# A two-layer graph network with experts on one Trainium2 core: the order around two reductions, and the first expert's first weights fetched for all experts

## The reference, cut to what matters

```python
kp = prm_exp(k, w)
qp = prm_exp(q, w)
D = jnp.einsum('btm,bm->bt', qp, jnp.sum(kp, axis=1))[..., None]
kptv = jnp.einsum('btn,btm->bnm', v, kp)
y = jnp.einsum('btm,bnm->btn', qp, kptv) / (D + EPS_ATTN)
y = v + (y @ proj_w + proj_b)
h2 = layernorm(y, n2_g, n2_b)
```

```python
logits = x @ Wg + bg
w, idx = jax.lax.top_k(logits, K)
w = jax.nn.softmax(w, axis=-1)
h = jax.nn.silu(jnp.einsum('bsh,ehf->ebsf', x, W1) + b1[:, None, None, :])
y = jnp.einsum('ebsf,efh->ebsh', h, W2) + b2[:, None, None, :]
comb = jnp.einsum('bske,bsk->ebs', jax.nn.one_hot(idx, E, dtype=x.dtype), w)
return jnp.einsum('ebsh,ebs->bsh', y, comb)
```

## Time and profile before

| | us |
|---|---|
| median of 3 runs | 827.68 |
| the three runs | 823.75, 831.24, 827.68 |
| profiled execution, device time | 823.53 |
| its span, first to last instruction | 821.7 |
| PE busy in the span | 792.5 (96%) |
| DVE busy | 533.9 (65%) |
| ACT busy | 251.2 (31%) |
| POOL busy | 142.5 (17%) |
| mean granted TensorE clock | 0.983 of full |

### The profile page before, as it was taken

The page is one execution under the profiler, slowest core; times in us unless marked ns, Lnnn a source line. Parts: engine busy times, 40 slices in busy tenths (PEclk is TensorE's granted clock), DMA queues, the critical chain, the costliest instruction groups (busy, mean ns, idle before and its releaser), DMA issues.

```text
span 821.7 us, 10813 instructions
## 1 busy us (share of the span) xinstructions
PE 792.5 (96%) x3983; PEld 634.0 (77%) x3983; DVE 533.9 (65%) x731; ACT 251.2 (31%) x488; POOL 142.5 (17%) x106
## 2 busy tenths in 40 slices
PE   5999999999999999999999999999599999999997
PEld 4998758766577776577858778898499989888886
DVE  6867999999999999985878445078531111511112
ACT  4452214245211014024143442133432321432310
POOL 3100010220200000001301620032342420442400
PEclk9999999999999999999999999999599999999999
DMA  7601789796987876711053110000342130423001
GB/s 247 235 1 52 223 250 347 219 273 217 255 325 252 276 246 232 233 58 50 1 165 104 53 51 0 1 1 1 103 161 95 52 103 0 135 70 102 0 0 62
DMA packets 60339, 107.89 MB, mean 131 GB/s; under 512 B 4065, under 2 KB 13662, under 8 KB 60300
## 3 DMA queue, kind: packets, MB, share of 16 engines
q1 hardware_dynamic: 54636, 96.97, 35.3%
q0 software_dynamic: 2880, 5.12, 3.8%
q10 hardware_dynamic: 2784, 5.27, 1.7%
HBM read 103.51 MB, written 1.28 MB: 128 GB/s over the span
## 4 chain that ended last, share of the span: by engine, by line
PE 93%; DVE 3%; issue 1%; ACT 1%; DVEq 0%; POOL 0%; DMA 0%; POOLq 0%; SPq 0%
PE bank L1341 55%; PE bank L1799 14%; PE bank L1410 6%; PE bank L1560 4%; PE bank L1579 3%; PE bank L1572 2%; PE bank L1553 2%; PE bank L1348 2%; PE bank L1667 2%; PE bank L1459 1%; PE bank L1742 1%; PE bank L1545 0%; ACT slot L617 0%; DVE tmp L953 0%; DVE slot L968 0%
## 5 line engine op out<-in xcount | busy, mean ns | idle before, releaser
L1040 DVE SCALAR_TENSOR_TENSOR weights<-weights,att 128x2048 f32<-128x2048 f32 x116 | 263.5, 2344 | 0.7
L1322 DVE CAST hid_hi<-slot 128x626 fp32r<-128x626 f32 x32 | 15.7, 492 | 159.2 <-ACT slot L894 159.2
L1341 PE MATMUL bank<-half,ew_hi 128*128 128x314 f32 (+1 forms) x512 | 112.9, 310 | 2.2 <-POOL ew_lo L586 2.2
L1341 PE MATMUL bank<-AT,slot 125*128 125x312 f32 (+1 forms) x400 | 105.8, 426 | 0.0
L1341 PEld LDWEIGHTS bank<-AT,slot 125*128 125x128 f32 x400 | 75.6, 189 | 30.4 <-issue 1.3
L586 POOL TENSOR_TENSOR ew_lo<-weights,ew_hi 128x1024 fp32r<-128x1024 f32 x28 | 69.2, 2492 | 133.3 <-ACT ew_hi L876 133.3
L1341 PEld LDWEIGHTS bank<-half,ew_hi 128*128 128x128 f32 x512 | 87.4, 191 | 5.6 <-issue 2.9
L1341 PE MATMUL bank<-weights,slot 128*125 128x512 f32 (+5 forms) x306 | 84.4, 437 | 0.7 <-ACT slot L775 0.7
L894 ACT ACTIVATE slot<-bank,eb_now 128x312 f32<-128x312 f32 x64 | 33.4, 523 | 155.3 <-PE bank L1341 155.3
L1341 PE MATMUL bank<-half,ew_lo 128*128 128x312 f32 (+1 forms) x256 | 78.9, 308 | 0.0
L1341 PEld LDWEIGHTS bank<-weights,slot 128*125 128x125 f32 (+2 forms) x306 | 50.2, 196 | 28.4 <-issue 24.7
(11 more groups left out here) (301 smaller groups left out, 1112.7 us busy)
## 6 DMA issues: line engine op xcount, KB each, us to landing
weights<-in_L_gnn_basis SPq DMA_DIRECT2D x60, 1024.0 KB, 5.4
weights<-in_L_ffn_W SPq DMA_DIRECT2D x32, 512.0 KB, 4.4
weights<-in_L_mix_kqv_w SPq DMA_DIRECT2D x1, 3072.0 KB, 10.3
weights<-in_w_qkvT SPq DMA_DIRECT2D x3, 1024.0 KB, 6.3
slot<-slot POOLq DMA_DIRECT2D x10, 250.0 KB, 7.2
weights<-in_L_mix_mlp_w ACTq DMA_DIRECT2D x2, 1024.0 KB, 17.1
weights<-in_L_gnn_root ACTq DMA_DIRECT2D x2, 1024.0 KB, 9.3
slot<-in_row_v_b POOLq DMA_DIRECT2D x5, 250.0 KB, 7.5
```

Source lines behind the costliest of these rows:

```text
L1040: ins = dve.scalar_tensor_tensor(wrel[layer][r], wmat(at), att[:, layer, r, b:b + 1], wrel[layer][r], ALU.mult, ALU.add)
L1341: ins = pe.matmul(out, a, b, start=i == 0, stop=i == len(pairs) - 1)
```

## The change

It has three parts.

1. **pv ahead of D.** PE makes the two pv banks before D; `PSUM_ORDER` says so too. DVE does sums 28 to 37 ahead of reading D, and none between D and the rows; sum 38 moves behind the rows.
2. **First W1 part of all experts in advance.** As soon as the q product of the attention in layer 1 is done, SP loads the first 256 columns of W1 for all eight experts, as 16 DMAs of 256 KB (512-byte pieces), into `candidates` (weights 2048 to 10239). To make room, Wo moves from 6144 to 10240, the split blocks of q and proj change places, and chunk c now lies in block (c + 3) mod 4 of the split weights. When the list is there, ACT reads the expert's number and makes the high half of the candidate in two parts of 128 columns (`first_high`); DVE reads it too and makes the low halves (`first_low`) right behind the one-hots, ahead of the softmax weights. DVE writes the list of experts in one instruction where it took three. PE starts with half of hidden block 0, then combT, then the other half, then eb2, then goes on from f = 1. SP loads no W1 chunk 0, and loads chunk 1 once `first_low` is 2. The first expert stands ahead of the loop on every engine, with an order of its own: ACT splits W2 of chunk 0 behind the Silu of f = 0, chunk 1 behind that of f = 1, chunk 2 behind f = 2, chunk 3 behind f = 3, then as before; DVE makes chunk 1's low half behind splitting hidden blocks 0 and 1. The rest of the experts (here one) stay in the loop, in the old order.
3. **Roots ahead of columns.** ACT's list becomes roots 0, 1, 2, columns 0, root 3, columns 1, root 4, columns 2, 3, 4.

The diff, cut:

```diff
 PSUM_ORDER = [
...
-              ("ks", 1), ("kptvA", 1), ("xdq", 1), ("kptvB", 1), ("qpT", 5), ("D", 1), ("pv", 2), ("proj", 5),
+              ("ks", 1), ("kptvA", 1), ("xdq", 1), ("kptvB", 1), ("qpT", 5), ("pv", 2), ("D", 1), ("proj", 5),
...
+        candidates = weights[:, 2048:2048 + 1024 * E1].rearrange("p (q f) -> p q f", f=128)
+        def chunk_block(c):
+            return (c + 3) % 4
+        def first_part(t, f):
+            return t[:, chunk_block(0), 0:1024].rearrange("p (k f) -> p k f", k=KT)[:, :, 128 * f:128 * f + 128]
...
-            sp.wait_ge(S("elist"), 1)
+            sp.wait_ge(S("psum_full"), filled("xq", 8))
             sp.wait_ge(S("lin_split"), 4)
             w1v = I["L1_ffn_W1"].rearrange("e (k p) f -> e p k f", p=128)
+            for e in range(E1):
+                for f in range(2):
+                    load(candidates[:, 8 * e + 4 * f:8 * e + 4 * f + 4, :], w1v[e, :, :, 128 * f:128 * f + 128], "cand_in")
+            sp.wait_ge(S("elist"), 1)
...
             for c in range(8):
-                if c >= 2:
+                if c == 1:
+                    sp.wait_ge(S("first_low"), 2)
+                elif c:
                     wait_split(sp, 0, c - 2)
-                load_chunk(e, c)
+                load_chunk(e, c, first=c == 0)
...
-            for j in range(TT + 1):
-                if j < TT:
-                    sqrt_of_tile("xe_row", 0, j)
-                if j:
...
+            sqrt_of_tile("xe_row", 0, 0)
+            sqrt_of_tile("xe_row", 0, 1)
+            sqrt_of_tile("xe_row", 0, 2)
+            xe_columns(0)
+            sqrt_of_tile("xe_row", 0, 3)
+            xe_columns(1)
+            sqrt_of_tile("xe_row", 0, 4)
+            for j in range(2, TT):
+                xe_columns(j)
             act.wait_ge(S("gap"), 2)
             act.activation(eexp, eexp, ACT.Exp).then_inc(S("gap_exp"), 1)
+            act.wait_ge(S("elist"), 1)
+            act.wait_ge(S("cand_in"), 16 * 2 * E1)
+            e = act.value_load(el_i[0:1, 0:1], min_val=0, max_val=E1 - 1)
+            for f in range(2):
+                act.activation(first_part(ew_hi, f), candidates[:, bass.ds(8 * e + 4 * f, 4), :], ACT.Copy).then_inc(S("first_high"), 1)
...
+            for f in range(16):
+                silu(0, f)
+                if f == 0:
+                    split_chunk(0, 0, parts=(1,))
+                elif f < 4:
+                    split_chunk(0, f)
+                elif f % 2 == 0 and f < 12:
+                    split_chunk(0, f // 2 + 2)
+            with act.Fori(0, n_act - 1) as rest:
...
-            sum_bases(0, 28, 35)
+            sum_bases(0, 28, 38)
             dve.wait_ge(S("psum_full"), filled("D", 1))
...
-            sum_bases(0, 35, 39)
...
-            sum_bases(0, 39, 2 * NB)
+            sum_bases(0, 38, 2 * NB)
...
-            link(dve.tensor_scalar(key1, srt, 1.0, -1.0, ALU.max, ALU.mult))
-            link(dve.tensor_scalar(key1, key1, float(E1), None, ALU.add))
-            dve.tensor_copy(el_i[0:1, 0:8], key1).then_inc(S("elist"), 1)
+            dve.tensor_scalar(el_i[0:1, 0:8], srt, -1.0, float(E1), ALU.mult, ALU.add).then_inc(S("elist"), 1)
...
             one_hots(U[0], E1, U[2:4], idx)
+            e = dve.value_load(el_i[0:1, 0:1], min_val=0, max_val=E1 - 1)
+            for f in range(2):
+                dve.wait_ge(S("first_high"), f + 1)
+                dve.tensor_tensor(first_part(ew_lo, f), candidates[:, bass.ds(8 * e + 4 * f, 4), :], first_part(ew_hi, f).bitcast(f32),
+                                  ALU.subtract).then_inc(S("first_low"), 1)
...
+            for f in range(16):
+                split_hidden(0, f)
+                if f == 1:
+                    second_chunk(0)
+            add_expert(0, e)
...
+            pe.wait_ge(S("first_low"), 1)
+            hidden(0, 0, 0)
             pe.wait_ge(S("comb"), 1)
...
+            hidden(0, 0, 1)
             pe.wait_ge(S("act_read"), READ0["combT"] + 2)
...
+            expert(0, 1)
+            with pe.Fori(0, n_act - 1) as rest:
+                expert(rest + 1, 0)
```

174 lines of the change are left out of this document (102 added, 72 removed), and 2 rows, old and new, of the table PSUM_ORDER.

## The result

The changed kernel takes 821.53 us (median of 20 runs, 818.86 to 823.63), the kernel before 828.01 us (20 runs, 823.20 to 831.59). The ratio is 0.9926 with a 95% interval of 0.9904 to 0.9947. The forecast was 822.7, range 816.5 to 829.0. The profiled executions are 820.29 and 823.53 us. The ratios in this document come from all runs, not from the two medians beside them, and lie near the quotient of the means (here 821.27 to 827.40). Where the groups described next are unevenly filled, that isn't the quotient of the medians.

The account below looks back on a forecast made before the run. PE, busy 792.5 of 821.7 us, bounds the kernel, so its waits and slow clock count. Terms -1.8 - 0.3 - 2.9 = -5.0 against the execution of 823.53 gave 818.5, carried over to the median as 822.7; range 816.5 to 829.

Parts of the forecast that it names:

- DVE's sums along: Attention of layer 0: DVE's moved sums end at 167.7, before the first proj bank at about 168.0, so DVE isn't late.
- The new wait: First expert, ahead of f = 2: PE waits about 1.8 us for chunk 1, queued behind Silus and copies.
- E + 5.3: First expert: f = 2 starts 5.3 us after E, the end of f = 1 forecast at 596.1.
- the sign that was named: Expected in the new profile: PE waits 1 to 2.5 us for DVE's low half of chunk 1 ahead of f = 2.
- W2's low half: Ahead of output(0): POOL's split of W2 chunk 0 ends at 595.4, just in time; an overrun up to 1.5 is covered.
- the Trainium skill's floor for such a load: PE's reading of the expert count before f = 1: about 600 ns; without cover, E (end of f = 1) 0.6 later.
- the 4.15 us: Whole kernel: the difference between profiled execution 823.53 and median 827.68, carried over from 818.5 to 822.7.
- A (no new wait, clock up early): Expert stretch: the wait doesn't bite, the clock rises early, f = 2 at 598.5; -8.6, 819.1 us; chance 0.15.
- B (low clock for longer): Behind the choice of experts: clock stays low longer, f = 2 at 602.9; -3.2, 824.5 us; chance 0.15.
- if the clock drops elsewhere in the shortened stretches: One of three signs that would make the prediction wrong, beside ACT waiting for candidates and PE for DVE in the attention.
- C (candidates late): Expert stretch: the sixteen candidate loads land after the list, f = 2 at 620.8; +14.4, 842 us; chance 0.05.
- D (part 2 nothing): Expert stretch: slow clock, slow DVE, uncovered load; f = 2 near 604.9, only part 1 left; 826.5 us; chance 0.10.

Follow-up runs that it names:

- wide pair: The kernel before, without and with pv ahead of D and DVE's sums moved, both with D, first gate and expert logits 64 columns wide: 822.08 and 819.90 us.
- old_sums: The changed kernel with DVE's sums as before and PE's new order kept: 831.62 us, ratio to the kernel before 1.0058.
- p3_alone: The kernel before with only ACT's roots moved ahead of the column copies: 829.55 us, ratio 1.001.
- wide kernels: The kernel before and the changed kernel, both with D, first gate and expert logits 64 columns wide: 822.08 and 817.11 us.
- wide_before: The kernel before with only the products of D, the first gate and the expert logits made 64 columns wide: 822.08 us, ratio 0.9935.
- p2_alone: The kernel before with only the candidates, first half blocks ahead, first expert unrolled and shorter list: 823.63 us, ratio 0.9951.
- p1_alone: The kernel before with only pv ahead of D and DVE's sums moved: 823.42 us, ratio 0.9957.

## Why the prediction was right, point by point

**Part 1** was given -1.8, with the waits of 1.07 and 0.69 as its size. It measured -2.2 in the timelines at proj (10.04 against 12.28, and 10.07 against 12.28 in the wide pair), and the wide pair keeps it up to the first neighbour products. The mechanism was right: both waits gone, proj behind D, DVE's row 0.23 us ahead of its bank. The sum was too small because it let pv and D last as long as their records. Products overlap: in the earlier trace rows D starts 1.07 us after the transposes' end and pv starts 0.13 before D's end. Where no wait stands in between, a group starts 0.14 to 0.17 before the modelled end of the one before it (156.57 against 155.50 + 1.23; 163.44 against 156.57 + 7.04). Against the forecast's 10.52 us from the transposes to proj (166.26 - 155.74), the measured 10.04 is 0.16 shorter at the transposes, 0.24 at pv and 0.08 at D. In this trace a wait that went gave back its length and that overlap.

**DVE's sums along** was costed at nothing, with the sums' end at 167.7 and the first bank at about 168.0. They came at 167.41 and 167.64. That the sums had to move was argued from the 170.05 us at which the old ones would end, and old_sums shows it, with 8 to 10 us.

**Part 3** was given -0.3 with bounds of +0.2 and -1.0; it is 0 in p3_alone, and PE's wait is 0.9 in all profiles. In the wide pair the list comes 0.36 us sooner against the transposes' start (577.0 - 156.2 against 577.0 - 155.8), which is the two instructions saved ahead of the list (0.38) and leaves nothing for the roots. The earlier root met a row scaling that the profile shows at 1.28 to 1.47 us beside POOL.

**Part 2** was given -2.9 at f = 2, with the 0.4 of the shorter list in it. It measured 2.9 from the list's instruction to the end of f = 2 (22.97 against 25.89) and 0.4 for the shorter list: -3.3. Step by step, each from the list's instruction: first product forecast 3.3, measured 3.7, DVE took 1.29 for two blocks of 512 columns as forecast (0.6 each); end of f = 1 14.6 and 14.3; f = 2 19.9 and 19.2. The clock came up 3.8 us after the first product, where 5 were taken and 2.9 was the bound. The new wait was forecast at 1.8 ahead of f = 2, "E + 5.3"; measured is E + 4.9, and PE's waiting is split, 0.8 ahead of output(0) and 0.4 ahead of f = 2, so the sign that was named, a wait of 1 to 2.5 us ahead of f = 2, came out too large. The 0.8 was foreseen as possible and put down to W2's low half; it was DVE's hid_lo, 0.81 us of work behind five additions of 3.08 us, and POOL was done at 594.3. That step named the wrong engine, at little cost. PE's reading of the count showed no wait, so the Trainium skill's floor for such a load (DMA: Bandwidth & Descriptors, Latency and other measured facts), which would have put f = 1 0.6 us later, was hidden behind eb2's products as the sum had it.

**The sum** was -5.0 for the execution. Taken from the timelines, part 1 at proj and part 2 behind the list, the parts give 2.2 + 3.3 = 5.5. No pair of times shows that number as it is. In the profiled pair the span fell by 4.2 us (821.7 to 817.5): 0.2 of it lies ahead of the transposes, 0.6 is what the clock left of part 1, 0.5 lies between the first neighbour products and the list (the shorter list is 0.4 of it), and 2.9 behind the list. The device time fell by only 3.2, since the changed kernel's execution took 2.8 us around its span and the other 1.8. Over 20 runs of the changed kernel this remainder is 1.7 to 3.4 us, over 30 of the kernel before 1.8 to 1.9; what lengthens it is open. The wide kernels' medians give just 5.0 (822.08 to 817.11), but their profiled spans differ by 4.6: 0.4 ahead of the transposes, 1.0 left of part 1 after the dip that wide_before lacks, 0.4 up to the list, 2.8 behind it. That the medians meet the forecast to a tenth is luck.

The medians of the kernels themselves give 6.5. The old order, in the executions at 831.34 (p3_alone) and 828.06 (p2_alone), has its first dip on D and pv (pv 9.92 and 9.61 us instead of 7.11), while no run of the changed kernel was over 823.63. The forecast carried the 4.15 us between before's execution and its median over unchanged. The changed kernel's own difference is 1.24, so this was the weak step: the forecast came within 1.2 us of the median because two errors cancelled (818.5 forecast and 820.29 measured for the execution, 4.15 and 1.24 for the way to the median). That part of the hit is luck.

**The rivals.** A (no new wait, clock up early) didn't happen: waits of 1.2 us, clock up after 3.8. B (low clock for longer) failed in the expert stretch, but the clock was low for longer in the attention, where the prediction had put no price on it. It had named that as a sign of being wrong ("if the clock drops elsewhere in the shortened stretches"), and by this sign it was wrong: 178.4 to 185.2 us at 0.50, before 182.3 to 185.7. C (candidates late) is out: about 290 GB/s, landed 18 us ahead of need. D (part 2 nothing) is out by the 2.9 us behind the list and by p2_alone.

## What to carry to other kernels

- Where an engine waits for another's copy in a chain of short products, put independent products into that place and move along what the third engine does in between. Here half of the edit (PE's order without DVE's sums) costs 8 to 10 us, the whole gains 2.2.
- Where PE's clock falls while PE is busy, look at what it was working on. Stretches of 1- to 8-column products cost the same time at 64 columns here, and with them wide the clock didn't fall there. Fill an unavoidable wait with redundant products if the clock falls in it.
- An agreement of two medians can be chance. Compare the starts of the same instructions through both timelines, and see where a gain arises and where it is lost again.
- When runs fall into groups, one profiled execution isn't the median. Profile executions of several groups, and compare their clock windows, before a few microseconds are put down to an edit.

## What the runs showed of the hardware that was not expected

- The granted clock fell to 0.50 with PE busy 7.99 of 8.00 us (178 to 186). The Trainium skill (TensorE: Matmul & The Clock Gate, HAM oscillation) puts such losses down to idle gaps of PE behind waits; this trace has none there, and what PE did before and in the fall was proj, 8 transposes and the gate's 40 products of 2 columns. With D and the gate 64 columns wide, all of 155 to 195 was at 1.00 in the profiled executions of all five kernels that have them so; in the nine others its mean was 0.78 to 0.96. Where it fell differs: in D (p3_alone, p2_alone), on proj right behind D (p1_alone, old_sums), in the gate (the changed kernel). Why narrow products should do this is open.
- 20 product records of D took 2.24 us at 1 column and 2.29 at 64, the gate's 40 4.43 us at 2 columns and 4.48 at 64, all at the high clock.
- The groups go with the clock: of two executions with spans 7.9 us apart, 5.0 us come from a stretch with PE fully busy but for two equal waits, and 1.2 from the first 160 products of the kernel, which took 23.26 and 24.44 us though the granted clock is printed as 1.00 in both.
- A dip at about 316 to 323 us (window 310 to 335 at 0.93) is in the profiled executions of thirteen kernels and absent in wide_before's (1.00); it costs 1.2 us. Right ahead of it stand two more groups of products of 2 columns (`gate_w`, 16 records at 304.3 and 24 at 316.1 us in the kernel before) that no run widened. They are as narrow in wide_before, so their width alone doesn't decide; widening them too is the test that is missing.
